# A gated delta-rule layer with a mixture of experts on one core: the output gate as one Silu on ScalarE, and a new order of the five instruction lists

## The reference

```
x = x + attention(layernorm(x))          # 8 heads of 128
x = x + experts(layernorm(x))            # top 2 of 8 experts, 128 -> 512 -> 128, relu

attention: q, k, v = conv4(x @ qkv_w)    # causal convolution of 4 taps per channel
           z = x @ z_w;  beta = sigmoid(..);  alpha = exp(-exp(A_log) * softplus(..))
           per token: S = S * alpha
                      S = S + k (v - k.S) * beta
                      o = q.S
           o = o * rsqrt(mean(o*o) + 1e-6) * norm_w
           o = o * (z * sigmoid(z))      # the output gate
           out = o @ out_w
```

## Time and profile before

| | us |
|---|---|
| median of 3 runs | 1410.39 (1410.18 to 1411.52) |
| the profiled execution | 1407.17 |
| its span in the trace | 1405.3 |
| from the first take-up of T to the 16th, 15 stages | 1023.4 |

### The profile page before, as it was taken

The page is one execution under the profiler, slowest core; times in us unless marked ns, Lnnn a source line. Parts: engine busy times, 40 slices in busy tenths (PEclk is TensorE's granted clock), DMA queues, the critical chain, the costliest instruction groups (busy, mean ns, idle before and its releaser), DMA issues.

```text
span 1405.3 us, 33741 instructions
## 1 busy us (share of the span) xinstructions
PE 1172.5 (83%) x11978; PEld 944.4 (67%) x11978; DVE 1167.0 (83%) x2531; ACT 834.4 (59%) x2536; POOL 710.7 (51%) x598
## 2 busy tenths in 40 slices
PE   0355989898989899898989899999898988469992
PEld 0233868686868686777777777777777777358881
...
DMA packets 163174, 97.07 MB, mean 69 GB/s; under 512 B 115623, under 2 KB 148269, under 8 KB 161988
## 3 DMA queue, kind: packets, MB, share of 16 engines
...
...
## 4 chain that ended last, share of the span: by engine, by line
DVE 32%; PE 26%; POOL 16%; issue 10%; DMA 7%; ACT 6%; SPq 2%; POOLq 0%; DVEq 0%; ACTq 0%
POOL kq L637 9%; DVE Y_sb L1056 7%; DVE blkT L1060 7%; PE kx L1541 3%; POOL decay L629 3%; POOL rows_in L609 2%; DMA blkN<-scr_n 2%; PE kx L1636 2%; POOL kq L620 2%; PE rc L1703 2%; DVE blkN L1047 2%; DVE Gs L1204 1%; DVE area L1146 1%; ACT Gs L836 1%; PE rc L1704 1%
## 5 line engine op out<-in xcount | busy, mean ns | idle before, releaser
L637 POOL TENSOR_TENSOR kq<-tapA,area 128x256 f32<-128x256 f32 x256 | 253.2, 1003 | 89.1 <-DVE area L1146 88.1
L758 ACT ACTIVATE area<-pj,taps 128x256 f32<-128x256 f32 x256 | 123.3, 482 | 138.8 <-PE pj L1555 130.4
L1056 DVE TENSOR_TENSOR Y_sb<-blkT,blkN 128x4 f32<-128x4 f32 (+18 forms) x304 | 172.4, 567 | 10.5
L1541 PE MATMUL kx<-kq 128*128 128x128 f32 x1024 | 143.1, 288 | 43.2 <-ACT area L767 32.6
L609 POOL DMA_INDIRECT rows_in<-rowbuf,dest x64 | 64.8, 1012 | 214.8 <-DVE dest L1132 187.3
L1541 PEld LDWEIGHTS kx<-kq 128*128 128x128 f32 x1024 | 130.2, 199 | 57.8 <-issue 41.2
L1143 DVE SCALAR_TENSOR_TENSOR tapA<-pj,taps,tapA 128x256 f32<-128x256 f32 x256 | 122.2, 477 | 51.7 <-ACT tapA L758 49.8
L620 POOL TENSOR_TENSOR kq<-kq,area 128x1024 f32<-128x1024 f32 x64 | 151.1, 2363 | 0.0
L1060 DVE TENSOR_REDUCE blkT<-Y_sb 128x2 f32<-128x4 f32 (+18 forms) x304 | 142.5, 469 | 5.2
L758 ACT ACTIVATE tapA<-pj,taps 128x256 f32<-128x256 f32 x256 | 123.1, 481 | 0.0
L1146 DVE SCALAR_TENSOR_TENSOR area<-pj,taps,area 128x256 f32<-128x256 f32 x256 | 121.4, 474 | 0.0
...
...
## 6 DMA issues: line engine op xcount, KB each, us to landing
...
scr_n<-area SPq DMA_DIRECT2D x128, 32.0 KB, 1.6
...
```

The source lines that it names most:

```text
L637: nc.gpsimd.tensor_tensor(dst[:, n % H, :], tapA[:, n % RING, :], tapB[:, n % RING, :], ALU.add).then_inc(conv_done, 1)
L758: ins = nc.scalar.activation(dst[:, n % RING, :], pj[n % 2][:, k:k + GT], ACT.Copy, scale=taps[:, t, k:k + 1])
L1056: ins = nc.vector.tensor_tensor(p4, bc(blkT[:, r0:, j:].rearrange("p r (o m) -> p r o m", o=1), [128, nr, w, wd]), bc(blkN[:, j:j + w, j:] ...
L1541: ins = mm(o, lhs[:, hh, cs], rhs_[:, hh, cs], start=True, stop=True)
```

## The change

ScalarE computes Silu(z) from the bank in one instruction and writes the finished gate; the VectorE step `zg` is gone from the code and from the order, and the semaphore between them with it. The output weights take the factor 1/256 in place of 0.5/64/256. ScalarE's step waits for `g` of the block before, since it overwrites the gate itself. The compiled list of ScalarE holds two more ACT_TABLE_LOAD, one ahead of the first Silu and one ahead of the exponential near the end of the experts.

```
-            for t in (z_tanh, kd_ready, rhs_ready, u_ready, sq_done, gn_ready, gt_ready):
+            for t in (zg_ready, kd_ready, rhs_ready, u_ready, sq_done, gn_ready, gt_ready):
...
                     elif step == "zt":
                         c, u = arg
+                        if g is not None:
+                            act.wait_ge(g_ready, halves(g, c, u))
                         act.wait_ge(z_mm, halves(a, c, u))
-                        nc.scalar.activation(zg[:, c, HU * u:HU * u + HU, :], heads(pj[u]), ACT.Tanh,
-                                             scale=0.5 / WSCALE).then_inc(z_tanh, 1)
+                        nc.scalar.activation(zg[:, c, HU * u:HU * u + HU, :], heads(pj[u]), ACT.Silu,
+                                             scale=1.0 / WSCALE).then_inc(zg_ready, 1)
...
-            nc.vector.tensor_scalar(ow[:, :, :], ow[:, :, :], nw[:, 0:1], 0.5 / WSCALE / VSCALE, ALU.mult,
+            nc.vector.tensor_scalar(ow[:, :, :], ow[:, :, :], nw[:, 0:1], 1.0 / VSCALE, ALU.mult,
...
-                    elif step == "zg":
-
-                        c, u = arg
-                        dve.wait_ge(z_tanh, halves(a, c, u))
-                        nc.vector.scalar_tensor_tensor(out=half(zg, c, u), in0=half(zg, c, u), scalar=1.0,
-                                                       in1=heads(pj[u]), op0=ALU.add, op1=ALU.mult).then_inc(zg_ready, 1)
```

ORDER is written anew; two of its lines:

```
-            sd.0.1 taps.14 g.0.0 o.0.1 first.13 ka.1 st.0.1 sq.0.1 proj.15 last.12 v.1.0 sm v.1.1 scale.0 bi ks.1.0 kd.0.0
+            last.12 taps.14 g.0.0 bi st.0.1 scale.0 proj.15 v.1.0 first.14 taps.15 first.15 inv.0 ktr.0.0 o.0.1 inv.1 inv.2
```

More of the change, by code:

```diff
@@ L249, in preln_delta_moe_kernel @@
         ORDER = """
-            proj.0 proj.1 taps.0 taps.1 diag.0 first.0 v.0.0 proj.2 m.1.0 taps.2 al.0 first.1 proj.3 m.0.0 last.0 taps.3
-            rdiag.0 me.1.0 v.0.1 first.2 proj.4 first.3 ka.0 last.1 me.0.0 m.1.1 taps.4 proj.5 me.1.1 ks.0.0 m.0.1 taps.5
-            scan.0 first.4 m.1.2 proj.6 me.0.1 rdiag.1 ks.0.1 last.2 last.3 first.5 me.1.2 proj.7 m.0.2 m.1.3 al.1 taps.6
-            diag.1 first.6 taps.7 last.4 proj.8 first.7 kk.0.0 me.0.2 me.1.3 m.0.3 last.5 proj.9 last.6 xl.0 rhs.0.0 me.0.3
@@ L264, in preln_delta_moe_kernel @@
-            st.1.1 xs.1 tj sc
+            ka.0 proj.0 taps.0 proj.1 first.0 v.0.0 proj.2 al.0 taps.1 m.0.0 taps.2 m.1.0 first.1 proj.3 taps.3 rdiag.0
+            diag.0 first.2 v.0.1 xl.0 first.3 scan.0 me.0.0 proj.4 proj.5 me.1.0 last.0 last.1 taps.4 taps.5 diag.1 m.1.1
+            me.1.1 first.4 first.5 ks.0.0 m.0.1 last.2 me.0.1 last.3 al.1 proj.6 taps.6 last.4 last.5 m.1.2 proj.7 rdiag.1
+            ks.0.1 me.1.2 m.0.2 m.1.3 first.6 last.6 taps.7 first.7 scan.1 last.7 kk.0.0 proj.8 me.0.2 me.1.3 nm.0.0 taps.8
@@ new lines, in preln_delta_moe_kernel @@
+            last.14 last.15 ue.1.0 u.1.1 aq.1 kq.0.0 inv.9 ue.1.1 ac.1 o.1.0 o.1.1 z.0.0 sd.1.0 inv.10 sd.1.1 ktr.0.1 inv.11
+            sq.1.0 sq.1.1 at.0.0 scale.1 inv.12 inv.13 kd.0.1 inv.14 ktr.1.0 rms.0 kd.1.0 inv.15 ktr.1.1 rms.1 kd.1.1 nr
+            inv.16 gn.0.0 g.1.0 kq.0.1 z.0.1 zt.0.0 gn.0.1 z.1.0 inv.17 gt.0.0 at.0.1 gt.0.1 gte.0.0 inv.18 g.1.1 xt zt.0.1
+            gte.0.1 xe lg gn.1.0 gn.1.1 inv.19 out.0 gt.1.0 rk gte.1.0 z.1.1 inv.20 gt.1.1 gte.1.1 inv.21 kq.1.0 pf tp x2.0
+            xl.1 zt.1.0 ps st.1.0 out.1 at.1.0 to x2.1 kq.1.1 st.1.1 xs.0 zt.1.1 at.1.1 sc ti tj xs.1
@@ L1015, in _ @@
             dve.wait_ge(s_zero, 1)
-            for t in (n_ready, at_ready, zg_ready, S_ready, g_ready):
+            for t in (n_ready, at_ready, S_ready, g_ready):
                 dve.sem_inc(t, HALVES)
```

17 lines of the change are left out of this document (6 added, 11 removed).

## The result

| | before | after |
|---|---|---|
| median, us (4 runs each) | 1410.95 (1410.18 to 1413.25) | 1439.11 (1436.99 to 1444.06) |
| ratio of the two | | 1.0215, interval 1.019 to 1.024 |
| profiled execution, us | 1407.17 | 1439.55 |
| its span, us | 1405.3 | 1437.7 |

The change makes the kernel slower by 28 us, 2.2% by the ratio. The forecast was 1423: the right side, and under half of the size (13 us of 28). 1439 lies inside the whole range (1380 to 1446) and above the forecast's own (1415 to 1434).

The account below looks back on a forecast made before the run. VectorE was taken to bound the inverse, T's transfers much of the stretch after it, TensorE and GpSimd the stretch before. Terms summed to +0.9 us per stage, about +15 with 15 stages and table load, rounded to 1423; range 1380 to 1446.

Parts of the forecast that it names:

- The gate products at 0: Between the inverse's end and the next T: removing 64 VectorE products gains 0 us per stage, bounds 0 and 2.4.
- a wait for T of 30 us or more: Sign in the changed profile: VectorE's wait ahead of T's transpose grows from 7.0 us to 30 or more.
- rival B: Much faster: the products' whole 2.4 us comes off each stage, giving 1372 us; chance 0.09.
- ScalarE's side at 0 and 1.3: On ScalarE: Silu for tanh makes no difference, and the second added table load, among the expert tiles, costs 1.3 us.
- first.15 at -0.8: Ahead of the inverse: two multiply-adds move out of it into idle time, saving 0.8 us per stage.
- The ranking at -0.5: Router's ranking on VectorE: its 0.87 us wait for the logits falls by 0.5 us per stage.
- GpSimd at +2.2: In the inverse: `sp` and three later GpSimd instructions collide with VectorE's small products, 4.35 for 2.15 us per stage.
- T to the inverse at +0.2: From T's arrival to the inverse's start: the new order costs 0.2 us per stage, bounds -1.5 and +2.
- Item 4: From T to the inverse: moved `ka.0`, `m.1.0`, `diag.1` and `ac.0` laid out together as +0.2 us per stage.
- The trip at 0: From the inverse's end to the next T: transfers set its 8.13 us, the change shortens none; 0 per stage.
- rival A: Faster: GpSimd collisions in the inverse cost no more than before; 1392 us, 1377 with an earlier inverse start; chance 0.28.
- Rival C: Slower: TensorE's chain from the norm to the inverse's export becomes the limit, 1 to 2 us per stage, 1440-1450; chance 0.12.

Follow-up runs that it names:

- silu_old_order: Kernel before the change, its order kept, without the four gate products and with Silu in place of tanh: 1415.77 us, ratio 1.0048 to before.
- tanh_new_order: Changed kernel's order with the old gate (tanh on ScalarE, product on VectorE): 1465.31 us, ratio 1.0395 to the kernel before.
- first15_back: Changed kernel with `first.15` moved back from ahead of `inv.0` to behind `inv.4`: 1441.75 us, ratio 1.0233 to the kernel before.
- the mirror: Kernel before the change with `aq.1` moved from ahead of `last.10` to behind `last.14`, in the inverse: 1433.97 us, ratio 1.0178 to before.
- xs0_behind_ti: Changed kernel with `xs.0` issued behind `ti` instead of between T's write and read: 1430.09 us, ratio 1.0165 to the kernel before.

## Why the prediction was right in sign and wrong in size

- **The gate products at 0.** Right in the main, by silu_old_order (0.2 to 0.7% slower, not faster). The sign it was to show by, a wait for T of 30 us or more, did not come (9.3). The freed time turned into VectorE's wait for `taps.0` behind ScalarE's stand at `tj` (L1144 above, 1.9 us a stage on average), which I had not looked for: rival B's sign and rival B's result are two different things.
- **ScalarE's side at 0 and 1.3.** No run gives the exchange of tanh for Silu in the stages by itself. The second load is 1.283 us long, as assumed, and the time from the first to the last send of the expert tiles is 131.8 to 132.0 us in every kernel with Silu and 131.2 to 131.3 in the three with tanh, so it costs some 0.6 us. The other 3.5 us behind the last T were in no term, and a tanh kernel has them too (the part ahead of the experts is 88.8 us in before, 92.4 in after and 93.6 in tanh_new_order).
- **first.15 at -0.8.** Wrong. It was counted as falling into idle time. But VectorE's idle time from T to the inverse is the same in both kernels (4.49 and 4.47 us a stage), and its work there is 0.4 more. Idle time there is mostly waits for ScalarE's copies, and the two multiply-adds did not fill it. first15_back shows the move at 0 to 3 us (ratio 1.0233 against 1.0215): the move had made the inverse 0.5 us shorter, not 0.8, and the parts on both sides of it 0.2 longer each.
- **The ranking at -0.5.** Right. Its wait fell from 19.7 to 11.1 us in all, 0.54 a stage.
- **GpSimd at +2.2.** The mechanism was right, down to the start of `sp.1` 2.5 us behind that of the inverse, and the mirror shows it in the other kernel. The size was too large. The small products lost 35.3 us (172.4 to 207.7), the large ones gave back 12.4 (L1047 21.8 to 11.5, L1043 14.7 to 12.6), so 22.9 / 16 = +1.43.
- **T to the inverse at +0.2.** This step failed, with 12 us. Measured +1.0: VectorE is ready 0.43 later, by `first.15`, and the read of the blocks is waited for 0.57 longer. Item 4 named the suspects (`m.1.0`, `ac.0`, `ka.0`), and none of them alone gives the start back. `m.1.0` and `ka.0` cover each other at the first scan, and `ac.0` costs ScalarE what it saves SyncE. The fourth, `diag.1` ahead of `last.2`, had no run; by the ring it is not the limit, since `last.3` ends 9.0 us behind T and `taps.7`, which waits for it, starts at 11.9. What makes the masks late stays open.
- **The trip at 0.** This step failed too, with 11 us. I called it transfers "and nothing that the change shortens" and did not ask what could lengthen it. Moving `xs.0` from between the write and the read took 0.64 us off (xs0_behind_ti). Moving `aq.1` took 0.5 off as well; by which way is not shown. And taking the products out brings the router's first send nearer to the write of T, by 1.2 us in silu_old_order, where the trip is 0.22 us longer: a removed instruction let something else start earlier. That the sends lengthen the trip is read from traces, not tested.
- **The sum.** With the measured contention the inverse is -0.8 - 0.2 - 0.54 + 1.43 = -0.1, measured +0.06. So +0.9 became +1.8 because the parts on both sides of the inverse were laid out as nearly unchanged. They cost 12 and 11 us more than laid out, the inverse 10 less, and what lies outside the stages 4 more; without the error in the inverse the forecast would have been further off. The low end of the range is also off: rival A with its earlier start was 1377, not 1380.
- **Rival C** is there in a small form: `gte.1.1` holds `tp` back in 4 of 16 blocks, by 1.89, 1.52, 1.34 and 0.85 us, or 0.35 us a stage at most. The time came out as rival C had it (1440), for other causes.
- **The signs.** "Over 1 us in three or four forms" held for one form in the means (128x64, 1215 ns), since the collision falls on another shape from stage to stage. "The inverse under 31" did not occur. The first part, which was to stay at 28.5 to 29.5 us, was 29.98; it changed by 1.0 us, the bound at which I had said the prediction fails. TensorE's longest wait was the one ahead of `z.1.0` in 8 of the 15 stages, and by its sum it is the longest (1.9 us a stage).
